# Attention on eight cores: the diagonal scale tiles built on VectorE, and the transpose evictions split 3 to 5 in place of 4 to 4

## The reference

```
q = x @ q_w.T + q_b          # 16 heads of 128
k = x @ k_w.T + k_b          # one head
v = x @ v_w.T + v_b          # one head
scores = q k^T / sqrt(128), causal mask
attn = softmax(scores)
x1 = layernorm(x + (attn @ v) @ o_w.T + o_b)
out = layernorm(x1 + (x1 @ (w * scale)^T + bias))
```

## Time and profile before

| what | value |
|---|---|
| median of the runs | 2345.68 us (2338.57 to 2347.38, 3 runs) |
| profiled execution, its own time | 2346.4 us |
| span of its slowest core (core 6) | 2344.8 us (cores 2327.8 to 2344.8) |
| TensorE busy, weight loads | 1522.3 us (65%), 667.2 us (28%) |
| VectorE (DVE) busy | 898.1 us (38%) |
| ScalarE (ACT) busy | 941.7 us (40%) |
| GpSimd (POOL) busy | 334.6 us (14%) |

### The profile page before, as it was taken

One profiled execution on the slowest core, in us unless ns is written; L12 is line 12 of the kernel. 1 busy time (PEld: TensorE's weight loads), 2 busy tenths in 40 slices (PEclk: granted clock), 3 DMA queues, 4 the chain that ended last, 5 costly groups with the idle time before them and its releaser, 6 DMA issues.

```text
span 2344.8 us, 25902 instructions; the slowest of 8 cores (2327.8 to 2344.8 us)
## 1 busy us (share of the span) xinstructions
PE 1522.3 (65%) x7077; PEld 667.2 (28%) x7216; DVE 898.1 (38%) x1985; ACT 941.7 (40%) x2334; POOL 334.6 (14%) x335
## 2 busy tenths in 40 slices
PE   0799953445555566665566656587968677777772
PEld 0344422222222222222233323332323222222221
DVE  0000003445555555555555555510534423235334
ACT  0111114655555555655555555532234121223421
POOL 0000010000000000000000000023445242444431
PEclk9999975656777577777677677798979898898886
DMA  9222299700000000000000000034523536442242
GB/s 142 39 39 43 36 100 109 107 1 1 1 1 1 1 1 1 1 1 1 1 1 1 1 1 1 1 117 122 165 74 106 137 108 179 128 151 89 81 162 90
DMA packets 43640, 137.06 MB, mean 58 GB/s; under 512 B 5835, under 2 KB 5868, under 8 KB 42988
## 3 DMA queue, kind: packets, MB, share of 16 engines
q1 hardware_dynamic: 28988, 84.02, 11.6%
q0 software_dynamic: 5296, 34.60, 11.2%
q10 hardware_dynamic: 9216, 16.78, 2.6%
HBM read 153.21 MB, written 33.55 MB: 80 GB/s over the span
## 4 chain that ended last, share of the span: by engine, by line
PE 35%; DVE 15%; ACT 15%; DMA 14%; issue 13%; POOL 3%; another core or an unknown queue 3%; DVEq 1%; ACTq 0%; POOLq 0%; SPq 0%
ACT expS L396 12%; PE psT L259 9%; DVE mpart L375 8%; DMA xres<-xT 8%; PE psT L836 4%; POOL ycs L797 3%; DMA outT<-outb 3%; PE psS L484 3%; PE psU L836 2%; PE psS L347 2%; PE psO L836 2%; DMA trib_s<-tri 2%; DVE expST L458 2%; PE psT L484 2%
## 5 line engine op out<-in xcount | busy, mean ns | idle before, releaser
L375 DVE TENSOR_REDUCE mpart<-psS 128x1 f32<-128x512 f32 (+3 forms) x327 | 190.4, 600 | 381.2 <-PE psS L356 371.9
L797 POOL TENSOR_TENSOR ycs<-yscr,xres 128x512 f32<-128x512 f32 x64 | 85.8, 1340 | 1433.6 <-ACT yscr L786 1273.4
L396 ACT ACTIVATE expS<-psS,negm 128x512 bf16<-128x512 f32 (+3 forms) x327 | 201.4, 619 | 218.3 <-DVE negm L379 217.4
L259 PE MATMUL psT<-xTbf,qwst 128*128 128x512 bf16 x1003 | 220.1, 379 | 1.3 <-ACT Vsb L241 0.2
L439 PE MATMUL psS<-diagP,expS 128*128 128x128 bf16 x1075 | 133.8, 259 | 98.6 <-ACT expS L396 59.0
L408 DVE TENSOR_REDUCE den<-dpart 128x1 f32<-128x2 f32 (+2 forms) x192 | 30.0, 156 | 414.3 <-ACT expS L396 414.3
L347 PE MATMUL psS<-KT,QTO 128*128 128x512 bf16 (+3 forms) x308 | 139.0, 471 | 69.0 <-ACT expS L396 54.1
L484 PE MATMUL psS<-expST,Vsb 128*128 128x512 bf16 x301 | 122.3, 547 | 86.0 <-ACT expST L463 54.5
L417 ACT ACTIVATE diagP<-ident_s,rcp 128x128 bf16<-128x128 bf16 x256 | 102.7, 401 | 144.4 <-DVE rcp L413 144.4
L836 PE MATMUL psT<-x1T,fwst 128*128 128x512 bf16 x500 | 127.3, 409 | 46.2 <-ACT x1T L720 29.1
L638 DVE TENSOR_SCALAR rowb<-psS 1x512 f32<-1x512 f32 x8 | 5.4, 681 | 395.6 <-PE psS L618 395.6
(11 more groups left out here) (111 smaller groups left out, 2573.1 us busy)
## 6 DMA issues: line engine op xcount, KB each, us to landing
wost<-wo_bf SPq DMA_DIRECT2D x64, 512.0 KB, 4.1
fwst<-fw_bf SPq DMA_DIRECT2D x64, 512.0 KB, 3.8
xres<-xT ACTq DMA_DIRECT2D x64, 256.0 KB, 3.9
outT<-outb SPq DMA_DIRECT2D x64, 256.0 KB, 3.6
xTbf<-xT POOLq DMA_DIRECT2D x1, 8192.0 KB, 63.0
qwst<-qw POOLq DMA_DIRECT2D x16, 512.0 KB, 5.1
wo_bf<-wo POOLq DMA_DIRECT2D x4, 2048.0 KB, 84.3
fw_bf<-fw POOLq DMA_DIRECT2D x4, 2048.0 KB, 102.9
```

The lines of the kernel that those rows point to most:

```text
L259: e.matmul(bk[:], qwst[:, (ot % 2) * D + dt * 128: (ot % 2) * D + dt * 128 + 128], xTbf[:, dt * S + c * W: dt * S + c * W + W], start=(dt ...
L375: mc=mcol + kc: e.reduce_max(mpart[:, mc:mc + 1], slot[:, 0:wdt], axis=AX.X),
L396: e.activation(expS8[:, (par * 4 + qt % 4) * S + kc * W: (par * 4 + qt % 4) * S + kc * W + wdt], slot[:, 0:wdt], AF.Exp, bias=negm8[:, nco ...
L797: pbuf=pbuf: e.tensor_tensor(pbuf[:, ot * W:(ot + 1) * W], yscr[:, (ot % 2) * W:(ot % 2) * W + W], xres[:, (ot % 3) * W:(ot % 3) * W + W], ...
```

## The change

Two edits, both in the attention stage. The diagonal tile is written by VectorE (`tensor_scalar` with a multiply by `rcp8`, bf16 in and out, all in SBUF) in place of ScalarE, and what waits for it waits on VectorE's counter. Of every eight transpose evictions, the first three go to ScalarE and the other five to VectorE; before, they alternated, VectorE first. Counted over the stage there are 256 diagonal tiles and 640 evictions, of which VectorE had 320 and then has 400. Each block begins with the counter at a multiple of eight.

```
-                E_diag2v[par][j] = p.op("scalar", lambda e, par=par, j=j,
-                                        ncol=ncol: e.activation(
+                E_diag2v[par][j] = p.op("vector", lambda e, par=par, j=j,
+                                        ncol=ncol: e.tensor_scalar(
                     diagP[:, (par * 4 + j) * 128:(par * 4 + j + 1) * 128],
-                    ident_s[:], AF.Identity,
-                    bias=0.0, scale=rcp8[:, ncol:ncol + 1]),
-                    waits=[E_rq, E_trmm2[par][j]], inc="a")
+                    ident_s[:], rcp8[:, ncol:ncol + 1], None,
+                    AluOpType.mult),
+                    waits=[E_rq, E_trmm2[par][j]], inc="v")
...
-                    eng = "vector" if trctr[0] % 2 == 0 else "scalar"
+                    eng = "scalar" if trctr[0] % 8 < 3 else "vector"
```

## The result

Over all runs the median went from 2344.46 us (10 runs) to 2435.44 us (9 runs). In some of them one die ran at a lower clock (up to 2505 us); the ratio of the other runs is 1.0384 with a 95% interval of 1.0348 to 1.042: slower by 82 to 98 us. The forecast was 2435, with a range of 2396 to 2466.

What follows compares the result with a forecast made beforehand. The prediction took a chain alternating between DVE and ACT as the bound. Tile 54, evictions 25 and block c = 0 10 us sum to 89 on 2346.4, so 2435 us; own range 2417 to 2466, range to hold 2396 to 2466.

Steps and rivals of the forecast that it cites:

- What bounds the stage: Attention stage, c = 1 to 3: DVE and ACT alternate; each microsecond added between sum and negated maximum lengthens the unit equally.
- What the tile saves on ScalarE: ACT in c = 1 to 3: losing 256 tiles only lengthens its wait ahead of exp; value 0.
- What the tile costs: DVE in c = 1 to 3: the tile adds 0.28 us to each of 192 units, +54 us (46 to 71).
- The handover: On DVE, the tile waits for the reciprocal and starts 0.26 us after it.
- The tile's duration: On DVE, the tile was taken to last 0.20 us, with bounds of 0.16 and 0.29.
- The evictions: DVE in c = 1 to 3: 15 steps a block of +0.21, +1.03 and +0.42 us, +25 us.
- Block c = 0: First block: PE path not shorter, DVE idleness filled; some 0.6 us a step, 16 steps, +10 us (0 to 24).
- block figures offered as a check: Attention stage: blocks longer by about 10, 17, 33 and 24 us for c = 0 to 3.
- ScalarE as the pace: Rival, ACT's handover from tile and evictions to exps: relieving ACT gives 111 us less, 2235; chance 0.06.
- late banks: Rival, c = 2 and 3: four DVE evictions in a row make PE's scores late; +64, 2499; chance 0.05.
- hidden work: Rival: PE paces the units and DVE's added work fills gaps; time stays at 2346; chance 0.05.
- The smaller loss: Rival: the tile starts without a handover gap; 23 + 25 + 4 = 52 us, 2398; chance 0.12.

Runs made afterwards that it cites:

- the tile alone: The kernel before with only the diagonal tile moved to VectorE, evictions alternating as before; ratio 1.033, stage 1232.3 us.
- the split alone: The kernel before with only the evictions split 3 to 5, the diagonal tile still on ScalarE; ratio 1.009, median 2355 us.
- the second profile of before: The kernel before profiled once more, no edit; stage 1163.9 us, part behind the stage 799.9 us.
- the constant column: The changed kernel with the tile scaled by a constant in place of the reciprocal, so it need not wait for it; ratio 1.0173, near 2373 us.
- with the tile on ScalarE: The kernel before with all 640 evictions on ScalarE, the tile staying there too; ratio 0.9487, 2214 us.
- 36.5 without: All evictions on ScalarE, the tile built on VectorE one unit later, behind the next unit's negated maximum; ratio 0.9265 against the kernel before.

## Why the prediction was right

**What bounds the stage: right.** DVE and ACT take turns, and what is added to DVE's turn is paid. Four runs tell it from the rivals: in c = 1 to 3 the tile costs 21 to 22 us a block where it stands in the turn and nothing where it stands in the wait, and ScalarE could be given 320 more evictions at a gain.

**What the tile saves on ScalarE: right, 0.** ACT's wait ahead of exp grew instead.

**What the tile costs: right in its make-up, too small in size.** 54 us forecast for c = 1 to 3, 65.8 measured with the tile alone. The handover was right (0.26 forecast, 0.27 measured). The tile's duration was not: 0.20 taken, 0.25 in the profile, inside the bounds of 0.16 and 0.29.

```profile
L417 DVE TENSOR_SCALAR diagP<-ident_s,rcp x256: 253/254/257, 362.5 to 1629.9; 128x128 bf16<-128x128 bf16 x128
```

Taking off half of the columns' price and a little more was one step too far. The Trainium skill ("VectorE: DVE Perf Modes", "The DRAIN you can't avoid") reports that a semaphore after each of eight tensor_copies costs nothing extra. This case differs: for the reciprocal and the tile, waiting for the instruction ahead costs 0.21 us.

**The evictions: right.** 25 us forecast for c = 1 to 3, 24.7 measured with the split alone. Each block is within 3 us of its own term, two below and one above, so that the total fits this well is in part luck.

**Block c = 0: right in the sum, 9.5 against 10.** The forecast said that the path through PE would not get shorter with both edits and that DVE's idleness would be filled. The changed kernel shows both: PE's product still starts 1.38 us behind the reciprocal, and the maxima's waits for PE are gone. But each edit alone moved c = 0 otherwise than its own expectation said, by 2.5 us in place of 10 and by -5.4 in place of a few more. So how the 10 us are put together is not confirmed, and that they met the 9.5 may be luck.

**Where the sum came out too well.** The terms gave 89 us and the whole kernel moved by 91, but the stage itself grew by 100: 9.5 + 24.2 + 35.4 + 29.0 and 2.0 between the blocks. The two profiles' other parts make up the difference, 7 us behind the stage and 2.5 ahead of it. Against the second profile of before, the part behind the stage is 3 us longer after the change, not shorter, so one execution's chance is enough for such a difference. But the 91 us are a difference of medians over ten and nine runs, and their interval, 82 to 98, does not reach 100: whether something outside the stage got shorter stays open. The step that was too small is the tile's term, by 12 us, and the match to the microsecond is luck. One of the block figures offered as a check also did not follow from its own terms: for c = 1, 18 + 15 x 0.21 is 21, not 17; measured were 24.2. For c = 3, 24 were offered and 29.0 measured.

**The rivals.** ScalarE as the pace and late banks are refuted for the changed kernel, and hidden work is for c = 1 to 3; in c = 0 the tile alone costs 2.5 us in all, of the 21 that 64 tiles would be. The smaller loss, a tile without a handover gap, is what the constant column produced: 1.0173, a stage 46 us longer than before, where the rival had 52.

## What to carry to other kernels

When no engine is near full, find the pair of engines that take turns, and ask of each instruction in whose turn it stands; busy shares alone would have moved this work in the wrong direction. The same instruction costs its full time in its engine's turn and nothing in its engine's wait, so try another place in the order before another engine. Relief by moving work to the other engine pays until that engine's wait has shrunk to zero: read that wait, block by block, as a bound of the gain. It is not the gain itself, since the moved work uses the wait up as well: in c = 1 ACT's wait was 67.9 us, and the gain 24.6 with the tile on ScalarE and 36.5 without.

## What was not expected of the hardware

On VectorE an instruction that waited for the result of the one ahead started 0.26 us (reciprocal behind the sum) or 0.27 us (tile behind the reciprocal) behind that one's start, an independent one 0.08 to 0.10, though the one ahead takes only 0.16: for this tile the dependence cost more than the work, 0.21 us against 0.12. The 128x128 two-byte tile took 254 ns with that wait, 245 where the instruction ahead was an unrelated one, and 235 with a constant scale; on ScalarE it took 401 ns and on GpSimd about 604.
